# Adaptive-layernorm block with token-choosing experts, one core: base sums, gathers and turns reordered around the one-hot search, and unread products on TensorE

## What is computed

```python
h = _layernorm(x) * (1 + cb) + sb                     # 4096 x 256
scores = softmax(h @ gate_w.T)                        # 8 experts
vals, idx = top_k(scores.T, 512)                      # each expert picks its 512 tokens
y = h[idx]; y = layernorm(y) * ln_w + ln_b
out = gelu(y @ fc1.T + b1) @ fc2.T + b2               # 256 -> 1024 -> 256, float32
h = h.at[idx].add(out * vals)                         # scatter-add
x = x + gb * h
```

## Time and profile before

| | before |
|---|---|
| median of 3 runs | 1499.42 us (1498.88 to 1502.54) |
| profiled execution, its own time | 1498.76 us |
| its span in the trace | 1496.7 us |
| mean granted TensorE clock | 0.974 |
| PE busy | 1433.8 us, 96% |
| DVE busy | 1199.9 us, 80% |
| ACT busy | 1062.3 us, 71% |
| POOL busy | 936.5 us, 63% |
| DMA, mean | 85 GB/s |

### The profile page before, as it was taken

The page is one execution under the profiler, slowest core; times in us unless marked ns, Lnnn a source line. Parts: engine busy times, 40 slices in busy tenths (PEclk is TensorE's granted clock), DMA queues, the critical chain, the costliest instruction groups (busy, mean ns, idle before and its releaser), DMA issues.

```text
span 1496.7 us, 44381 instructions
## 1 busy us (share of the span) xinstructions
PE 1433.8 (96%) x16356; PEld 1127.9 (75%) x16356; DVE 1199.9 (80%) x3694; ACT 1062.3 (71%) x2295; POOL 936.5 (63%) x1549
## 2 busy tenths in 40 slices
PE   8999999999999999999999999999999657999997
PEld 4556888888888888888888888888888445676675
DVE  6859999999999999999999999999989794223222
ACT  4558888888888898888988888888886851112211
POOL 4338787877778778787778777787785003234222
PEclk9999999999999999999999999999999758999999
DMA  7364121221212212123221222212354514345331
GB/s 242 131 211 130 34 63 37 82 67 42 63 36 78 58 54 63 37 71 82 65 63 36 67 56 67 63 34 65 91 148 118 171 64 156 89 97 163 94 81 21
DMA packets 100065, 126.90 MB, mean 85 GB/s; under 512 B 30132, under 2 KB 81444, under 8 KB 97800
## 3 DMA queue, kind: packets, MB, share of 16 engines
q1 hardware_dynamic: 92394, 113.06, 25.6%
q0 software_dynamic: 6480, 9.29, 3.4%
q10 hardware_dynamic: 974, 1.71, 0.3%
HBM read 93.83 MB, written 30.16 MB: 83 GB/s over the span
## 4 chain that ended last, share of the span: by engine, by line
PE 84%; DVE 6%; ACT 3%; issue 3%; DMA 1%; SPq 1%; POOL 1%; another core or an unknown queue 0%; POOLq 0%; DVEq 0%
PE pbank L970 27%; PE pbank L985 18%; PE pbank L956 15%; PE pbank L1435 7%; PE pbank L1445 7%; PE pbank L635 2%; DVE region_x L1048 2%; PE pbank L1289 2%; ACT region_x L1016 1%; PE pbank L650 1%; ACT region_c L1011 1%; DVE region_p L1614 1%; PE pbank L1350 1%; PE pbank L617 1%; SPq L193 0%
## 5 line engine op out<-in xcount | busy, mean ns | idle before, releaser
L956 PE MATMUL pbank<-region_s 128*128 128x512 bf16 (+3 forms) x1280 | 399.8, 349 | 4.3 <-DVE maxima L1048 3.5
L970 PE MATMUL pbank<-ident,region_a 128*128 128x128 f32 x2048 | 328.7, 274 | 2.8
L970 PE MATMUL pbank<-ident,region_x 128*128 128x128 f32 x2048 | 329.4, 273 | 0.9 <-POOL region_x L1088 0.9
L1080 POOL TENSOR_SCALAR region_x<-region_x,maxima 128x1664 f32<-128x1664 f32 (+3 forms) x128 | 202.4, 1581 | 174.7 <-ACT region_x L1016 171.5
L970 PEld LDWEIGHTS pbank<-ident,region_a 128*128 128x128 f32 x2048 | 254.9, 141 | 41.8 <-ACT region_c L1011 10.2
L1048 DVE CUSTOM_DVE_ANT_0 region_x<-pbank,region_t,maxima 128x512 f32<-128x512 f32 (+1 forms) x416 | 269.1, 699 | 17.0 <-PE pbank L956 17.0
L970 PEld LDWEIGHTS pbank<-ident,region_x 128*128 128x128 f32 x2048 | 252.1, 141 | 28.7 <-ACT region_o L1011 6.5
L1011 ACT ACTIVATE region_p<-pbank 128x512 f32<-128x512 f32 x384 | 224.1, 608 | 67.7 <-PE pbank L970 67.6
L1011 ACT ACTIVATE region_o<-pbank 128x512 f32<-128x512 f32 x448 | 266.4, 617 | 0.1
L1016 ACT ACTIVATE region_x<-region_x 128x384 f32<-128x384 f32 (+1 forms) x512 | 246.8, 508 | 0.0
L1048 DVE CUSTOM_DVE_ANT_0 region_a<-pbank,region_t,maxima 128x512 f32<-128x512 f32 (+1 forms) x352 | 230.6, 694 | 18.6 <-PE pbank L956 18.6
(11 more groups left out here) (223 smaller groups left out, 2351.2 us busy)
## 6 DMA issues: line engine op xcount, KB each, us to landing
region_t<-factor_rows SPq DMA_DIRECT2D x16, 1024.0 KB, 5.5
region_s<-q_split SPq DMA_DIRECT2D x256, 64.0 KB, 2.3
region_s<-k_split SPq DMA_DIRECT2D x256, 64.0 KB, 2.3
region_x<-in_fc_t SPq DMA_DIRECT2D x16, 1024.0 KB, 8.1
q_split<-region_o SPq DMA_DIRECT2D x16, 384.0 KB, 2.6
k_split<-region_t SPq DMA_DIRECT2D x16, 384.0 KB, 2.7
heads_out<-region_o SPq DMA_DIRECT2D x256, 16.0 KB, 1.5
region_c<-heads_out SPq DMA_DIRECT2D x16, 256.0 KB, 5.0
```

The source lines that it names most:

```text
L956: nc.tensor.matmul(score_ps[bank_of(s)][:, 0:(hi - lo) * P], stacks[:, b, 0, t * P:(t + 1) * P], stacks[:, b, 1, lo * P:hi * P], start=Tru ...
L970: last = nc.tensor.transpose(turn_ps[(h * NR + j) % TB][:, q * P:(q + 1) * P], rows[t][:, k * P:(k + 1) * P], ident[:, :])
L1080: nc.gpsimd.tensor_scalar(row, row, maxima[:, 4, n:n + 1], 1.0, ALU.add, ALU.mult).then_inc(shifted_pool, 1)
```

## The change

It is in `mixture` only.

- **Banks.** `base_ps` gets one bank for each of the 16 pairs from the list `BASE_BANK`; banks 5 and 7 (which hold what `find` sums) join for pairs 12, 13 and 15. `pairs_out_of(banks, before)` gives how many sums have to be done for these banks to be free.
- **PE.** Pairs 5 and 6 leave their places at the finds; pairs 5 to 13 come behind the spread. `turn_first` comes next, behind a wait for the sums of banks 0 and 1 alone (9 of them), then pairs 14 and 15, then a wait for those of banks 2 and 3 (12), then the experts. Expert 0 waits for all 16 sums ahead of its fc2 products.
- **Unread products.** `keep_up(count)` issues bfloat16 products of 128x128 by 256 columns into columns 256 to 511 of bank 6, which nothing reads: 18 ahead of find(0), behind a wait for `high_ones(0)`, and 20 between find(0) and find(1).
- **Spread.** 4 products of 32 columns instead of 8 of 16 columns.
- **DVE.** Sums 0, 1, 2 leave the one-hot chain: the one-hots of half 1 follow those of half 0 at once, then the indices, sum 0, save_indices, split_sides, sums 1 to 13, `normed_in` of expert 0, sums 14 and 15.
- **SP.** The stores of `out` wait for the 4 gathers of expert 0 to have landed.

```diff
+    BASE_BANK = (2, 3, 0, 1, 4, 2, 3, 0, 1, 4, 2, 3, 5, 7, 4, 5)
+    base_ps = [bank[i][:, :].rearrange("p (t d) -> p t d", d=D) for i in BASE_BANK]
+    PAIRS, PB = len(BASE_BANK), 5
+    def pairs_out_of(banks, before):
+        return max((p + 1 for p in range(before) if BASE_BANK[p] in banks), default=0)
...
+        for c in range(EC):
+            sp.wait_ge(gathered_first[c], 16)
         for g in range(G):
...
         def gate_pair(p):
-            if p >= PB:
-                pe.wait_ge(base_done, p - PB + 1)
+            if pairs_out_of((BASE_BANK[p],), p):
+                pe.wait_ge(base_done, pairs_out_of((BASE_BANK[p],), p))
...
+        def keep_up(count):
+            for _ in range(count):
+                nc.tensor.matmul(bank[6][:, 256:512], same_expert, o["bconst"][:, C_SAME:C_SAME + 256], start=True, stop=True)
+
+        pe.wait_ge(high_done, 1)
+        keep_up(18)
         pe.wait_ge(onehot_done[0], 3)
         for t in range(NT):
             find(0, t)
-        gate_pair(PB)
+        keep_up(20)
         pe.wait_ge(onehot_done[1], 3)
         for t in range(NT):
             find(1, t)
-        gate_pair(PB + 1)
         spread_indices()
-        for p in range(PB + 2, PAIRS):
+        for p in range(PB, PAIRS - 2):
             gate_pair(p)
...
+            if e == 0:
+                pe.wait_ge(base_done, PAIRS)
...
-        pe.wait_ge(base_done, PAIRS)
+        pe.wait_ge(base_done, pairs_out_of((0, 1), PAIRS))
         turn_first()
+        for p in range(PAIRS - 2, PAIRS):
+            gate_pair(p)
+        pe.wait_ge(base_done, pairs_out_of((2, 3), PAIRS))
...
         high_ones(0)
         with_tiles(0)
         low_ones(0)
-
-        add_base(0)
         high_ones(1)
         with_tiles(1)
         low_ones(1)
-        add_base(1)
         for a in range(QA):
             indices(a)
-        add_base(2)
+        add_base(0)
         save_indices()
         split_sides()
-        for p in range(3, PAIRS):
+        for p in range(1, PAIRS - 2):
             add_base(p)
...
         normed_in(0, 0)
+        for p in range(PAIRS - 2, PAIRS):
+            add_base(p)
```

More of the change, by code:

```diff
@@ L1151, in mixture @@
     h2_ps = proj_ps
-    base_ps = [bank[i][:, :].rearrange("p (t d) -> p t d", d=D) for i in (2, 3, 0, 1, 4)]
-    PAIRS, PB = NT // 2, len(base_ps)
+    BASE_BANK = (2, 3, 0, 1, 4, 2, 3, 0, 1, 4, 2, 3, 5, 7, 4, 5)
[3 more added lines that the diff above has]
+        return max((p + 1 for p in range(before) if BASE_BANK[p] in banks), default=0)
     found_ps = [bank[i][:, 0:2 * HIGH].rearrange("p (s r) -> p s r", s=2) for i in (5, 7)]
-    spread_ps = bank[6][:, P:2 * P].rearrange("p (a q r) -> p a q r", q=QE, a=QA)
+    spread_ps = bank[6][:, P:2 * P].rearrange("p (q a r) -> p q a r", q=QE, a=QA)
     y_ps, fc1_ps, fc2_ps = bank[0:2], bank[2:4], bank[4:6]
@@ L1349, in gate_pair @@
                 for k in range(KC):
-                    last = nc.tensor.matmul(base_ps[p % PB][:, i, k * P:(k + 1) * P], h2t[:, g, k, t * P:(t + 1) * P],
+                    last = nc.tensor.matmul(base_ps[p][:, i, k * P:(k + 1) * P], h2t[:, g, k, t * P:(t + 1) * P],
                                             gated_ident[:, g // GB, k, :], start=True, stop=True)
@@ L1394, in spread_indices @@
             pe.wait_ge(scaled_ident, B * KC + QE)
[L1395 to L1398, removed]
+            for q in range(QE):
+                last = nc.tensor.matmul(spread_ps[:, q, :, :].rearrange("p a r -> p (a r)"),
+                                        spread_ident[:, q, :, :].rearrange("p j l -> p (j l)"),
+                                        idx_f[:, :, :].rearrange("p a r -> p (a r)"), start=True, stop=True)
             last.then_inc(idx_spread, 1)
+        def keep_up(count):
[3 more added lines that the diff above has]
+        keep_up(18)
         pe.wait_ge(onehot_done[0], 3)
@@ L1662, in add_base @@
             pair = xs[:, 2 * p:2 * p + 2, :]
-            nc.vector.tensor_tensor(pair, pair, base_ps[p % PB], ALU.add).then_inc(base_done, 1)
+            nc.vector.tensor_tensor(pair, pair, base_ps[p], ALU.add).then_inc(base_done, 1)
         def high_ones(a):
@@ L1690, in save_indices @@
                 nc.vector.tensor_copy(idx_all[mine, :, :].rearrange("p (a q) c -> p a q c", a=QA),
-                                      spread_ps[mine, :, :, j * EC:(j + 1) * EC]).then_inc(idx_done, 1)
+                                      spread_ps[mine, :, :, j * EC:(j + 1) * EC].rearrange("p q a c -> p a q c")).then_inc(idx_done, 1)
         def split_sides():
```

## The result

| | before | changed |
|---|---|---|
| median of 10 runs | 1500.35 us (1498.88 to 1502.54) | 1495.28 us (1492.62 to 1496.85) |
| ratio | | 0.996, 95% interval 0.9952 to 0.9968 |
| profiled execution, its own time | 1498.76 us | 1492.62 us |
| its span | 1496.7 us | 1490.5 us |
| PE busy | 1433.8 us | 1418.6 us |

The kernel is faster, but by less than half of what the sum said, and 0.8 us outside the range.

A forecast was written before the change was run, and what follows sets the result against it. The chain that ended last was taken as the bound: time won ahead of 1259.07 us, where TensorE alone follows, counts. Gains of 1.75 + 0 + 1.85 + 5.8 + 2.2 = 11.6 us took 1498.76 to 1487.2; range 1484.5 to 1494.5.

The forecast's parts named there:

- Part 1: One-hot chain on DVE: with sum 0 gone from between the halves, find(1) can start earlier; gain 1.75 us.
- Part 2: Unread products around find(0): the 18 cost nothing, the 20 take 2.1 us and end as find(1) is ready; gain 0.
- Part 3: find(1): taken at 4.08 us as before, gain 0; bound 2.04 if the array limits it, 3.2 by the skill page.
- Part 4: From the end of find(1) to save_indices: 1.65 us instead of 3.51, gain 1.85.
- Part 5: From save_indices to the first fc1 product: 12.05 us instead of 17.88, TensorE's pairs setting the pace; gain 5.8.
- B: Rival: the clock falls during find(0), slowing the 20 unread products, spread and some two pairs; 4.9 us, 1492.1; chance 0.20.
- Part 6: Expert 0's fc1 products at the full clock: 13.73 us instead of 15.92, gain 2.2, or 0 if the clock falls.
- Part 7: Queues: SP's later stores, POOL's wait for them and SP's loads for expert 2 cost nothing.
- C: Rival: late signals under the burst of stores strike a handoff as fc1 starts; 4 us come back, 1491.2; chance 0.17.
- F: Rival: hardly any gain, B and C together with D on top; 1498.5; chance 0.07.
- D: Rival: expert 0's gathers land late and the turn's last two transposes wait 2.4 us; 1489.6; chance 0.06.
- E: Rival: slower, the store burst makes expert 0's fc1 handoffs late by 2.15 us each; all 8 make 1504.4; chance 0.05.

The follow-up runs named there:

- stores taken away: Changed kernel with SP's stores of the base waiting until DVE has scaled expert 0's rows, so none run beside pairs 6 to 13; 1493.36 us, ratio 0.9954.

## Why the prediction was wrong, point by point

- **Part 1 was right.** The one-hots of half 1 end 1.68 us earlier, counted from the turn of the places (1217.00 to 1233.54 before, 1216.48 to 1231.34 after; 1.75 was said). That the turn itself came 0.52 us earlier isn't the change's doing: from one profile to the next it moved between 1216.0 and 1219.0.
- **Part 2 failed in its price.** The 20 took 2.79 us in the chain, not 2.1, as the clock was at 0.50 until 1230.22. I had written that the cover ended just there and that a low clock would cost 2.2; find(1) started 0.6 late here and 0.8 to 1.3 in the other traces.
- **Part 3 was right.** find(1) ran wholly in a stretch at 1.00 and took 4.05 us, as long as at 0.50, so the array's clock doesn't set its pace. By the Trainium skill (TensorE: Matmul & The Clock Gate, "Wait — 56ns, not 53.3ns?") the floor is about 25 ns from start to start, which made my 3.2 us. The trace doesn't come down to it: 4.05 us for 128 products are 32 ns each.
- **Part 4** measured 1.93 us (1236.04 to 1237.97) for 1.65; the spread took 1.45 of it, as the clock fell at 1237.05, where it took 1.08 at the full clock (stores taken away).
- **Part 5 is the step that failed**: 16.85 us for 12.05. The run with `gather(1)` behind the turn parts it: without late signals 13.98 remain, so these took 2.87 of the profile (one trace each; 3.7 by the ratios). The other 1.93 are the clock: it was low until 1243.88, pairs 5 to 13 took 11.44 us (TensorE's records from 1237.75 on), as their first three ran at 0.50, and with or without late signals they ended 1.7 to 1.9 us later than the sum had it; from the turn to fc1 the run took 2.76 us for 2.7. The step that failed is the reading of the waits: I took the late signals of the earlier trace rows to belong to the stores and to vanish as the sums ran ahead of them, and booked 4.1 us as won. They belonged to the gathers, which the change leaves as they were. The sum also took the clock as full in all pairs; that it could fall stood only in B.
- **Part 6 was right**: 13.97 for 13.73, gain 1.95 for 2.2. The clock stayed full though TensorE was not without a break: it was idle for 0.27, 0.44, 0.47 and 1.08 us between 1250.2 and 1254.8.
- **Part 7 was right**: SP's issues grew from 0.38 us (median, before) to 1.45 us at most, and nothing on the chain waited for the stores; POOL did, until 1262.78, where it then put out expert 2's gathers.
- **The rivals.** Of B came the low clock, at 2.8 us instead of 4.9: 1.9 in the pairs, 0.6 at the 20, 0.3 at the spread. For it I had called the stretch from 1225.74 on nearly all find; it held 8.08 us of find in 13.35. Of C came the waits, at 2.9 us instead of 4.0, but neither its cause (the stores) nor its place (fc1). I had given the two together 0.07 (F), and only with D on top. Without D they make 1487.2 + 4.9 + 4.0 = 1496.1, and 1495.28 was measured; that this is near is luck, as both prices were too high and the trace behind the sum lies 1.6 us below its median. E and D did not come: the turn started when TensorE was free.
- **The profile closes.** 2.87 (late signals), 1.93 (clock in the pairs), 0.6 (the 20), 0.28 (part 4) and 0.24 (part 6) make 5.9, less 0.5 as the turn of the places came earlier: 5.4. The profiled execution took 1492.62 where the sum said 1487.2.
- **So do the books on a chip without late signals.** There the 4.1 us of part 5 can't be won, which leaves 7.5 of 11.6. The changed kernel's own trace there has find(1) 1.06 late, 12.58 for the 12.05 of part 5 and 13.97 for 13.73: 5.7 are left, and 1494.65 to 1489.08, 5.6, was measured. The kernel before has no trace there, so that its waits are missing is inferred from its time.

## What to carry to other kernels

A wait whose releaser had long been done (here TensorE's records ended 3.8 us ahead of the last sums) is a cost with a cause of its own: find that cause before booking the wait as gone, since reordering the waiters doesn't remove it. Work that fills an idle engine is only free if it ends early enough at the slower of two clocks. On a chip with late signals, moving a prefetch that nobody needs yet (expert 1's gathers) behind the work on the critical path was worth as much as the whole reordering. And chips differ: the same program took 1494.7 us on one and 1500.9 on another, so a cause found on one kind has to be looked for on the other.

## What the runs showed of the hardware that I had not expected

- With 6 or 8 indirect DMAs in a row on GpSimd, VectorE's starts behind TensorE were held up to 8.5 and 11.4 us after the first had started; with 4 in a row no wait was seen past 6 us. This was so on the chips on which the kernel before takes about 1500 us (six traces with 8, one with 6); on one with 1494.7 even 8 did nothing (one trace). It costs the unchanged kernel 5.5 us, about the difference between the chips.
- 128 products of 32 columns with 32-column weights took 4.0 to 4.1 us at either clock. The clock fell at 1237.05, just behind find(1), though TensorE had been busy for 6.33 of the 6.83 us before.
- 8 products on all 128 columns of the array, put among find(1)'s products on 32, lengthened it from 4.05 to 6.99 us.
- SyncE's issue of a 512 KB store took 0.40 us for the first of a burst and 1.06, 1.43 and 1.45 us for the third to the fifth (changed kernel).
